# A block of attention, time mixing and two expert layers on one core: squares on ScalarE, early moments of x, the tile map in two parts, and gathers released by another engine

## What is computed

```
x = x + xattn(layernorm(x), ctx)      # one head over 257 past and 32 own keys, LoRA weights
x = x + attn(layernorm(x))            # time mixing (a scan over tokens), then 8 experts, 2 of them a token
x = x + ffn(layernorm(x))             # a shared GEGLU and 8 expert GEGLUs, 1 of them a token
```

```
xk_e = ei * mk + shift(ei) * (1 - mk);  xr_e = ei * mr + shift(ei) * (1 - mr)
k_e  = square(relu(xk_e @ eWk));        kv_e = k_e @ eWv;      r_e = sigmoid(xr_e @ eWr)
```

## Time and profile before

| | us |
|---|---|
| median of 3 runs | 944.83 (944.80 to 945.19) |
| the profiled execution, whole | 948.37 |
| its span in the trace | 946.3 |
| PE busy | 863.0 (91%) |
| VectorE busy | 457.3 (48%) |
| ScalarE busy | 316.4 (33%) |
| POOL busy | 342.7 (36%) |

### The profile page before, as it was taken

The page is one execution under the profiler, slowest core; times in us unless marked ns, Lnnn a source line. Parts: engine busy times, 40 slices in busy tenths (PEclk is TensorE's granted clock), DMA queues, the critical chain, the costliest instruction groups (busy, mean ns, idle before and its releaser), DMA issues.

```text
span 946.3 us, 18950 instructions
## 1 busy us (share of the span) xinstructions
PE 863.0 (91%) x6360; PEld 774.4 (82%) x6360; DVE 457.3 (48%) x1355; ACT 316.4 (33%) x714; POOL 342.7 (36%) x580
## 2 busy tenths in 40 slices
PE   5899988887767789999967999999999999999998
PEld 4567767665666679999957999999999999999998
DVE  1269988889873565555535666621111111111114
ACT  1366767665453334444421111111111111111110
POOL 1444677775876336654313333010001100000033
PEclk9899999998589889999997999999999999999999
DMA  9775457435512222253311122065898989998114
GB/s 353 262 265 211 162 161 246 124 118 207 167 40 63 52 63 84 82 174 126 79 42 54 57 67 68 12 245 207 322 318 304 308 325 318 306 323 288 56 52 134
DMA packets 92110, 162.00 MB, mean 171 GB/s; under 512 B 13832, under 2 KB 71112, under 8 KB 88680
## 3 DMA queue, kind: packets, MB, share of 16 engines
q1 hardware_dynamic: 71008, 103.39, 32.6%
q10 hardware_dynamic: 12832, 37.82, 10.6%
q0 software_dynamic: 8176, 19.57, 7.8%
HBM read 146.10 MB, written 14.66 MB: 170 GB/s over the span
## 4 chain that ended last, share of the span: by engine, by line
PE 65%; DVE 13%; POOL 6%; DVEq 6%; issue 5%; DMA 3%; ACT 1%; ACTq 1%; another core or an unknown queue 0%; SPq 0%; POOLq 0%
PE bank L1635 27%; PE bank L1648 14%; PE bank L372 7%; PE bank L399 7%; PE bank L386 3%; DMA xz<-in_x_dram 2%; DVEq L1388 2%; PE bank L361 1%; DVE arena_b L1191 1%; POOL tab_e L685 1%; PE bank L779 1%; DVE arena_b L1211 1%; DMA arena_a<-rows_y,slot 1%; PE bank L1618 1%; DVE arena_b L501 0%
## 5 line engine op out<-in xcount | busy, mean ns | idle before, releaser
L1635 PEld LDWEIGHTS bank<-arena_b,arena_a 128*128 128x128 f32 x1472 | 168.0, 192 | 1.2
L1635 PE MATMUL bank<-arena_b,arena_a 128*128 128x128 f32 x1472 | 168.1, 275 | 0.0
L1701 ACT ACTIVATE arena_b<-bank 128x512 f32<-128x512 f32 x78 | 46.6, 597 | 301.0 <-PE bank L1635 301.0
L1843 DVE TENSOR_TENSOR arena_b<-bank,arena_b 128x512 f32<-128x512 f32 x78 | 54.0, 692 | 190.8 <-PE bank L1635 186.0
L1635 PE MATMUL bank<-arena_b,a_x 128*128 128x128 f32 x1024 | 122.6, 280 | 0.0
L1635 PEld LDWEIGHTS bank<-arena_b,a_x 128*128 128x128 f32 x1024 | 119.6, 196 | 0.4
L328 POOL DMA_INDIRECT arena_a<-rows_e,pick x78 | 76.0, 975 | 29.5 <-issue 29.5
L372 PE MATMUL bank<-arena_b,arena_a 128*128 128x128 f32 x624 | 82.2, 289 | 4.2 <-DVE hT L509 4.2
L1648 PE MATMUL bank<-arena_a,arena_b 128*128 128x256 f32 x368 | 83.2, 379 | 0.0
L372 PEld LDWEIGHTS bank<-arena_b,arena_a 128*128 128x128 f32 x624 | 78.6, 205 | 5.0 <-DVE arena_b L501 2.9
L1539 POOL COPY pick<-list_i 128x1 uint32 x23 | 4.2, 182 | 206.6 <-PE bank L1618 180.5
(11 more groups left out here) (275 smaller groups left out, 1365.8 us busy)
## 6 DMA issues: line engine op xcount, KB each, us to landing
arena_a<-in_W_dram SPq DMA_DIRECT2D x69, 1024.0 KB
arena_a<-in_ctx_n_dram ACTq DMA_DIRECT2D x16, 1152.0 KB
arena_a<-in_ctx_t_dram SPq DMA_DIRECT2D x16, 1028.0 KB
rows_y<-arena_a ACTq DMA_DIRECT2D x39, 128.0 KB
arena_a<-in_w_moe_dram ACTq DMA_DIRECT2D x3, 1156.0 KB
arena_a<-in_w_moe_dram ACTq DMA_DIRECT2D x3, 1152.0 KB
rows_f<-arena_b ACTq DMA_DIRECT2D x23, 128.0 KB
rows_e<-arena_b SPq DMA_DIRECT2D x64, 32.0 KB
```

The costliest lines, as they stand in the source:

```text
L1635: last = nc.tensor.matmul(bank[half][:, f * P:(f + 1) * P], w12[:, i, k, col0:col0 + P], zT[:, k], start=k == 0, stop=k == KD - 1)
L1701: nc.scalar.activation(act_g[:, half], bU[half][:], ACT.Gelu).then_inc(g_ac_g, 1)
L1843: nc.vector.tensor_tensor(hT_f[:, u % 2, half * HH:(half + 1) * HH].rearrange("p f t -> p (f t)"), bG[half][:], act_g[:, half], ALU.mult). ...
```

## The change

Four things change.

1. `squared(n)` on VectorE is gone. ScalarE takes the square of its own relu instead, from SBUF to SBUF, between relu and sigmoid of the tile. PE's down(n) waits for that (`m_asq`), and PE's hidden(n) for the relu of the tile before (`m_arelu`) where it waited for the square, since the relu is now the last reader of the bank.
2. `gather(n)` on POOL waits for receptance(n - 3) (`m_pr`) where it waited for the blends of tile n - 3 (`m_dx`).
3. The moments of x: groups 3 to 11 are taken in batches of 1, 2, 3 and 3 at the ends of steps 1 to 4, and steps 2 to 10 take none in their old place. The old places of steps 0, 1 and 11 to 14 stay.
4. `tile_map` is cut: `tile_counts` reads the totals before mixture step 6, and the rest, still called `tile_map`, stands behind mixture step 6. Mixture step 5 now goes ahead of both.

```
-                need(pool, m_dx, n - NM + 1)
+                need(pool, m_pr, n - NM + 1)
...
-                need(pe, m_dsq, n)
+                need(pe, m_arelu, n)
...
-                pe.wait_ge(m_dsq, n + 1)
+                pe.wait_ge(m_asq, n + 1)
...
                 act.wait_ge(m_ph, n + 1)
-                need(act, m_dsq, n - 1)
                 nc.scalar.activation(h_relu[:, n % 2], bMH[:], ACT.Relu).then_inc(m_arelu, 1)
+                need(act, m_py, n - 1)
+                act.wait_ge(m_arelu, n + 1)
+                nc.scalar.activation(hT[:, n % 2], h_relu[:, n % 2], ACT.Square).then_inc(m_asq, 1)
...
-            def squared(n):
-                dve.wait_ge(m_arelu, n + 1)
-                need(dve, m_py, n - 1)
-                nc.vector.tensor_tensor(hT[:, n % 2], bMH[:], h_relu[:, n % 2], ALU.mult).then_inc(m_dsq, 1)
...
-            def tile_map():
-                left = NT1 - TA
+            def tile_counts():
                 dve.wait_ge(pe_tot, 1)
...
                 nc.vector.tensor_tensor_scan(t_end[:], ones_e[:], n_tiles[:], 0.0, ALU.mult, ALU.add)
+
+            def tile_map():
+                left = NT1 - TA
                 dve.drain()
...
+            AHEAD = (3, 4, 6, 9, 12)
             for s in range(STEPS):
                 a, b, c, t = live(s), live(s - 1), live(s - 2), live(s + 1)
+                if 2 <= s < AHEAD[-1] - 1:
+                    t = None
...
-                if s == STEPS - 1:
-                    tile_map()
+                if 1 <= s < len(AHEAD):
+                    for n in range(AHEAD[s - 1], AHEAD[s]):
+                        stats0(n)
+                    dve.drain()
+                    for n in range(AHEAD[s - 1], AHEAD[s]):
+                        moments0(n)
                 if s >= MOE_AT:
                     moe(s - MOE_AT)
+            tile_counts()
             for m in range(STEPS - MOE_AT, MSTEPS):
                 moe(m)
+                if m == STEPS - MOE_AT:
+                    tile_map()
```

More of the change, by code:

```diff
@@ L121, in perceiver_block @@
         rs_2 = sb("rs_2", [P, G])
-        st0, mv0, rs0 = (sb(n, [P, 2, w]) for n, w in (("st0", 6), ("mv0", 2), ("rs0", 3)))
+        st0, mv0, rs0 = sb("st0", [P, 4, 6]), sb("mv0", [P, G, 2]), sb("rs0", [P, 2, 3])
         st1, mv1, rs1 = (sb(n, [P, 2, w]) for n, w in (("st1", 6), ("mv1", 2), ("rs1", 5)))
@@ L261, in perceiver_block @@
         m_pa, m_pr, m_ph, m_py, m_ap, m_asig, m_arelu, m_awk = sems1("m_pa m_pr m_ph m_py m_ap m_asig m_arelu m_awk")
-        m_dd, m_dx, m_dsq, m_dy, m_mu, m_gap = sems1("m_dd m_dx m_dsq m_dy m_mu m_gap")
+        m_dd, m_dx, m_asq, m_dy, m_mu, m_gap = sems1("m_dd m_dx m_asq m_dy m_mu m_gap")
         m_got = [sem1(f"m_got{i}") for i in range(NM)]
@@ L519, in step @@
                     mixed(m)
-                if 0 <= m - 1 < NT1:
-                    squared(m - 1)
                 if 0 <= m - 2 < NT1:
@@ L625, in rstd0 @@
                 need(pool, ac_hn, n - 1)
-                nc.gpsimd.tensor_scalar(r[:, 0:1], mv0[:, n % 2, 1:2], EPS, None, ALU.add).then_inc(po_r0, 1)
+                nc.gpsimd.tensor_scalar(r[:, 0:1], mv0[:, n, 1:2], EPS, None, ALU.add).then_inc(po_r0, 1)
                 pool.wait_ge(po_r0, 3 * n + 1)
@@ L629, in rstd0 @@
                 pool.wait_ge(po_r0, 3 * n + 2)
-                nc.gpsimd.tensor_scalar(r[:, 2:3], mv0[:, n % 2, 0:1], -1.0, r[:, 1:2], ALU.mult, ALU.mult).then_inc(po_r0, 1)
+                nc.gpsimd.tensor_scalar(r[:, 2:3], mv0[:, n, 0:1], -1.0, r[:, 1:2], ALU.mult, ALU.mult).then_inc(po_r0, 1)
             def rstd1(n):
@@ L1141, in stats0 @@
                 dve.wait_ge(ld_x[part], 16)
-                nc.vector.bn_stats(st0[:, n % 2], xz[:, n])
+                nc.vector.bn_stats(st0[:, n % 4], xz[:, n])
             def moments0(n):
-                nc.vector.bn_aggr(mv0[:, n % 2], st0[:, n % 2]).then_inc(dv_st0, 1)
+                nc.vector.bn_aggr(mv0[:, n], st0[:, n % 4]).then_inc(dv_st0, 1)
             def own_value(n):
```

## The result

| | before | after |
|---|---|---|
| median of 4 runs | 945.01 (944.80 to 945.28) | 960.00 (958.46 to 961.33) |
| span of the profiled execution | 946.3 | 956.7 |
| VectorE busy | 457.3 | 437.8 |
| ScalarE busy | 316.4 | 337.5 |
| PE busy | 863.0 | 864.3 |

The changed kernel is slower: ratio 1.0158, 95% interval 1.0140 to 1.0175, or 15 us. The forecast was 954.8, with a range of 947 to 964. The direction and the mechanism were right, and the size was two thirds of what was measured. The two profiled spans differ by 10.4 us, close to the sum of +10.0, but the medians differ by 15.0. That gap of 5 us turned out to be a fault in what the sum was set against: the profiled execution of before was not an ordinary one.

What follows compares the result with a forecast made beforehand. TensorE, 91% busy, was taken to bound most, with VectorE level in steps 5-9 and POOL's queue pacing steps 19-24. Terms -0.6 - 1.0 + 18.7 - 8.1 + 1 = +10.0 gave 958.4 profiled, 954.8 us median, range 947 to 964.

Steps and rivals of the forecast that it cites:

- The gather's wait: Pipeline steps 19 to 24: gathers waiting for receptance close a lap through POOL's queue, norm_out and PE; +18.7 us.
- the subtraction: At the totals product: predicted start 326.4 in place of the profiled 307.65, giving +18.7 us.
- Predict 3.5 below, as the median is.: Last step of the sum: 958.4 for the profiled execution, less 3.5 because the median lay that far below; 954.8 us.
- The map in two parts: From totals to turn(9): mixed(5) goes ahead and gather(9) is late next, 15.0 in place of 23.1; -8.1 us.
- Squares: Row numbers ahead of PE's L372: blends end one product sooner, -0.6 us; hidden on ScalarE, worth nothing in steady tiles.
- Moments: Steps 5 to 10: moments taken early relieve VectorE and POOL; sum -1.1, taken as -1.0 us.
- The cost of the batch ahead of step 5: End of step 4: three pairs ahead of L1208, from which VectorE is dense, cost 1.35 us.
- five steps count, 2.05: Steps 5 to 9: each saves 0.41 us of VectorE's moments and aggregate, 2.05 us together.
- Steady gathers: From tile 9 on: 1.6 us of slack holds except where 3 MB of weights come in; +1 us.
- The wait comes free: Rival at gather(3) to gather(5): POOL arrives no earlier than receptance or is idle behind; 935.1 us, chance 0.08.
- The lap is shorter: Rival in the laps: fewer VectorE squares and full PE clock bring three laps to 11.5 us; 943 to 947, chance 0.05.
- steady gathers late as well, 965: Rival in the steady part: landings of 5.0 us make tiles 5.2, 28 tiles cost 10 more; 965 us, chance 0.12.

Runs made afterwards that it cites:

- second trace of before: The kernel before, unchanged, run and traced once more as a yardstick: median 943.38 us, ratio 1.0008, span 941.3 us.

## Why the prediction was right, and where not

**The gather's wait: mechanism right, absolute times right, price wrong.** The prediction put receptance(0) to (3) at 275.2, 291.2, 306.2 and 319.5 and the totals at 326.4. POOL's gathers behind them started at 276.35, 291.59, 307.31 and 320.78, and the totals stood at 326.98: laps of 15.2, 15.7 and 13.5 us where the prediction had 16.0, 15.0 and 13.3. The step that failed is the subtraction: 326.4 minus 307.65. The 307.65 of the earlier trace rows came from an execution in which ScalarE and VectorE had stood still for a reason that the profile doesn't show, in the very stretch that the lap replaces. The ordinary value is 301.4 to 304.4 (seven traces without the early wait), so the wait costs 22.5 to 24.5 us from ranks(12) to the totals, not 18.7.

**"Predict 3.5 below, as the median is."** The last step of the sum took the 3.5 us between the profiled execution and the median to be spread over the program and to stay. They weren't: they sat in the replaced stretch, and went with it. Taken with the second trace of before, the parts add up to 956.7 - 941.3 = 15.4: +24.6 to the totals, -7.9 to turn(9), -3.0 to turn(12), +1.6 behind, and +0.1 for the two ends. The medians differ by 15.0. Against the first trace the same cuts give +19.6, -7.6, -2.9, +1.6 and -0.4, the 10.4 (10.3 with the rounding) of the spans, with which the +10.0 agreed so well. The agreement of the two spans would have hidden the error. The range held the result because its upper part had been set for other reasons, a slow clock in the laps and late landings. Two additions of the prediction are slightly off: 319.5 + 1.9 + 4.8 is 326.2, not 326.4, and the upper end of its bounds comes to 963, not 962; neither matters here.

**The map in two parts: right.** -8.1 predicted; -7.5 in the traces against the second one of before, -6.9 in the times. Turn(9) came 15.4 to 15.9 us behind the totals, for 15.0. In seven of the eight traces with the map in two parts what was late is what was named, gather(9): its turn waited 0.65 to 1.22 us for the rows. Such a row is the first here, from the kernel with the gather's wait undone. In after, whose rows follow, gather(9) did wait 3.24 us for its row numbers, but its turn at 342.43 waited for nothing and came only 0.1 us later than a tile of 4.82 us; there the 0.62 us belong to turn(7), whose gather had stood behind the last lap:

```profile
319.12 0.66 PE L361 MATMUL bank<-ident,arena_a 128*128 128x128 f32 x4 [1.18 <-DMA arena_a<-rows_e,pick]
...
332.64 0.66 PE L361 MATMUL bank<-ident,arena_a 128*128 128x128 f32 x4 [0.62 <-DMA arena_a<-rows_e,pick]
...
337.63 0.19 POOL L325 COPY mu_e<-late 128x4 f32 x1 [3.24 <-DMA pick<-tab_e]
...
342.43 0.66 PE L361 MATMUL bank<-ident,arena_a 128*128 128x128 f32 x4
```

**Squares: -0.6 predicted, some -2.5 measured.** The square takes 0.63 us on ScalarE, as taken, and hides. The turn (2.90 us late in after, 2.62 in before) and the four blends behind it are what is late next at the row numbers, as said. The term left out what comes behind. PE's stop ahead of L372 there is 0.59 us in place of 1.10, and the L372 then took 2.05 us in after where they had taken 3.75; turn(11) to turn(12) fell from 8.9 to 5.7:

```profile
356.40 2.05 PE L372 MATMUL bank<-arena_b,arena_a 128*128 128x128 f32 x16 [0.59 <-DVE arena_b L503]
...
355.00:360.00 5.00, 4.23 (x28) 3.83 (x29) 2.98 (x11) 2.86 (x5) 0.19 (x1) 1.00 0.07 1
```

The last row is a window of after; the granted clock is 1.00, the 2.4 GHz level. In before it was 0.53 from 343 to 350, nearly all at 1.2 GHz. It isn't so in each execution: of the eight traces with squares on ScalarE three have 2.05 us there and five 2.94 to 3.62. From turn(9) to turn(12) the eight have a mean of 19.4, the five with VectorE's squares 21.0, so in the changed kernel the squares are worth 1.6 on the average, more of it clock than wait. Alone they seem to gain at PE's stop behind the totals as well (21.1 to turn(9), in one trace, where the four with VectorE's squares and the old map take 22.0 to 23.3), which the cut map takes away.

**Moments: -1.0 predicted, 0 to -0.1 measured.** The cost of the batch ahead of step 5 was 0.63 where 1.35 was predicted, but the steps gave back 0.65 in place of 2.45. The step that failed is "five steps count, 2.05". From one group's reciprocal to the next, from step 5 on, after takes 11.90, 11.90, 13.35 and 13.20 where before took 12.30, 12.65, 12.86 and 12.84: a gain of 1.15 in two steps, and 0.85 of it lost in the next two. The prediction named PE's slack as what could eat the gain. VectorE in step 8 shows two more ways. This is after:

```profile
102.98 0.69 DVE L1206 TENSOR_TENSOR_SCAN arena_b<-arena_b 128x255 f32<-128x255 f32 x1
104.10 0.17 DVE L1246 MAX8 top<-logits 128x8 f32<-128x8 f32 x1 [0.44 <-ACT logits L1075]
104.19 0.67 DVE L1210 TENSOR_TENSOR_SCAN arena_b<-arena_b 128x255 f32<-128x255 f32 x1
...
105.92 0.54 DVE L1252 TENSOR_TENSOR hot<-iota_e,top_at 128x16 f32<-128x16 f32 x1
```

and this is before:

```profile
103.46 0.69 DVE L1211 TENSOR_TENSOR_SCAN arena_b<-arena_b 128x255 f32<-128x255 f32 x1
...
104.19 0.67 DVE L1215 TENSOR_TENSOR_SCAN arena_b<-arena_b 128x255 f32<-128x255 f32 x1
...
105.92 0.17 DVE L1257 TENSOR_TENSOR hot<-iota_e,top_at 128x16 f32<-128x16 f32 x1
```

The first scan is 0.48 us earlier, then VectorE waits 0.44 for the router's logits, and the second scan starts at 104.19 in both. Then a small operation takes 0.54 in place of 0.17, beside POOL's numerator, which runs from 105.59 in after and from 105.94 in before: the numerator starts 0.35 us earlier, near the 0.4 that POOL's readier rstd0 was to bring, and the operation beside it loses 0.37. That POOL's work caused it is read from the overlap and wasn't tested by itself.

**Steady gathers: +1 predicted, +1.6 to 1.9 measured,** at the named place (where the weights come in) and by the named mechanism (a landing later than the slack). The prediction gave a fit of the Trainium skill (DMA: Bandwidth & Descriptors, Anatomy of one DMA, SWDGE path) by which the term would have been +0.5. The traces side with the longer landings: in the second trace of before the 78 gathers took 2.7 us at least, 3.3 in the middle and 5.7 at most. So the prediction's own 2.74 was the short end, and with 3.3 the slack is 6.4 - 2.1 - 3.3, an estimate of 1.0 us, not 1.6.

**The rivals.** "The wait comes free" would have given 935.1; the kernel with the gathers a step later in the queue took 938.67, which is the case in which that rival holds. Its -9.7 for the rest of the change came out, 934.14 against 943.91 with the wait undone, but by luck: the moments brought nothing and the squares more than their 0.6. "The lap is shorter" and "steady gathers late as well, 965" didn't come.

## What to carry to other kernels

A wait in an in-order queue costs what stands behind it. Tied to an event of the next step it cost 24 us; with the gathers one step further down the queue the same wait cost nothing there. So before a wait is made stricter, compare where it stands with when its event comes, and move the waiting instruction along with it.

A sum against one profiled execution holds only if that execution is ordinary in the stretch that the change replaces: look there for idle times whose releaser is unknown, take them out first, and don't let the difference to the median ride along as a constant. When a predicted and a measured span agree, check the medians as well.

A saving on an engine that shares the pace with others has to be followed for some steps: here 1.15 us won in two steps had shrunk to 0.3 two steps on.

## What was not expected of the hardware

PE's clock made the laps dearer. From 270 to 327 us in after the mean granted clock was 0.71; in the same part of the second trace of before, 269 to 302, it was 0.93. Behind PE's idle times of 7.36 and 5.40 us the sixteen L372 took 3.62 us in place of 1.95. The first of the two, after, by window (the clock is the 0.50, the 1.2 GHz level):

```profile
302.00:306.00 4.00, 4.00 (x20) 4.00 (x19) 1.76 (x7) 1.85 (x5) 0.00 (x0) 0.50 0.01 4
```

How much of the 24 us is clock wasn't measured by itself; in after, L361, L372 and L386 together take 2.5 us more in mixture step 3 than in a steady tile (0.60, 1.95 and 1.03 us), and 2.7 in step 4. By these two steps alone an estimate is 5 of the 24 us.

Two engines stood still for 1.6 to 3.8 us at a time in one traced execution and in no other, with their inputs ready ([3.39 <-remote] and [3.77 <-remote] above). And the executions of one program spread over 0.8% on these chips (939.7 to 947.4), though the first four of before had agreed within 0.05%: a short row of equal times is no proof that the next will be equal. The spread goes with PE's mean granted clock: of the 65 executions of the kernel before, the four with 0.969 or more took 939.7 to 940.7 us, and the nineteen with 0.957 or less 944.7 to 947.4. What sets that clock from one execution to the next stays open.
